# Two attention layers over one context: Gram matrix of each context made in layer 0, kept in DRAM and loaded by layer 1

## What is computed

```python
# layer 0: text = ctx[:, :77], ip = ctx[:, 77:]
text_probs = softmax((x @ Wq) @ (text @ Wk).T * scale)
q_sem = text_probs @ text                       # [q, 512]
sem = q_sem @ ip.T * scale                      # = text_probs @ (text @ ip.T) * scale
fused = scores_ip + 0.5 * sem                   # the same sem for every head
...
# layer 1: text = ctx[:, :252], ip = ctx[:, 252:]
qsem = l2norm(probs_t @ text)                   # per head; probs_t: [h, q, 252]
ip_n = l2norm(ip)
sem = qsem @ ip_n.T
fused = attn_scores + 0.5 * sem
```

## Time and profile before

| | before |
|---|---|
| median of 3 runs | 1670.71 us |
| profiled execution: its span, first to last instruction | 1665.6 us |
| distance of the median from that span | 5.1 us |
| TensorE matmul busy | 1599.7 us (96%), 14248 matmuls |
| VectorE busy | 1376.6 us (83%) |
| ScalarE busy | 992.3 us (60%) |
| GpSimd busy | 844.8 us (51%) |
| moved by DMA | 175.31 MB, 105 GB/s on average |

### The profile page before, as it was taken

The page is one execution under the profiler, slowest core; times in us unless marked ns, Lnnn a source line. Parts: engine busy times, 40 slices in busy tenths (PEclk is TensorE's granted clock), DMA queues, the critical chain, the costliest instruction groups (busy, mean ns, idle before and its releaser), DMA issues.

```text
span 1665.6 us, 42402 instructions
## 1 busy us (share of the span) xinstructions
PE 1599.7 (96%) x14248; PEld 1424.2 (86%) x14248; DVE 1376.6 (83%) x3937; ACT 992.3 (60%) x2044; POOL 844.8 (51%) x789
## 2 busy tenths in 40 slices
PE   6999999999999999998989999999999999999986
PEld 5888888888888888788878998989998989998866
DVE  4688788888888888867879998999999998998874
ACT  3455565555556555655656666666666666666651
POOL 3224422222222323424767676777667776777662
PEclk9999999999999999999999999999999999999988
DMA  8334444444444444542323332333233323332201
GB/s 223 97 105 121 129 121 124 124 129 125 120 129 124 124 128 122 144 123 75 112 88 87 100 95 80 102 106 99 66 109 102 100 67 101 101 103 63 79 22 43
DMA packets 204225, 175.31 MB, mean 105 GB/s; under 512 B 45441, under 2 KB 203531, under 8 KB 204011
## 3 DMA queue, kind: packets, MB, share of 16 engines
q1 hardware_dynamic: 204010, 172.60, 35.8%
HBM read 112.13 MB, written 60.38 MB: 104 GB/s over the span
## 4 chain that ended last, share of the span: by engine, by line
PE 88%; DVE 6%; issue 3%; DMA 1%; SPq 1%; ACT 1%; POOL 0%; DVEq 0%; POOLq 0%; ACTq 0%
PE MISC L103 26%; PE GP L103 20%; PE NAT L265 10%; PE TR L278 8%; PE PV L324 5%; PE PV L309 4%; PE PV L306 3%; PE PV L327 2%; PE MISC L227 2%; PE MISC L367 1%; DVE ZP L895 1%; PE MISC L368 1%; PE MISC L466 1%; DVE TMP L779 1%; PE MISC L388 1%
## 5 line engine op out<-in xcount | busy, mean ns | idle before, releaser
L540 ACT ACTIVATE P<-TA 128x512 f32<-128x512 f32 x320 | 202.6, 633 | 279.4 <-DVE TA L888 278.0
L984 POOL TENSOR_TENSOR ZS<-ZP 128x256 f32<-128x256 f32 x267 | 255.4, 957 | 210.4 <-DVE ZP L895 209.0
L265 PE MATMUL NAT<-KS,QS 65*128 65x256 f32 x1280 | 300.1, 317 | 3.6 <-DMA KS<-qk_parts 2.1
L103 PE MATMUL GP<-PH,GH 128*128 128x256 f32 (+1 forms) x960 | 248.8, 288 | 20.9 <-DVE ZP L895 19.9
L278 PE MATMUL TR<-QS,KS 69*128 69x256 f32 (+1 forms) x1280 | 259.9, 285 | 4.6 <-DMA QS<-max_rows 2.5
L783 DVE TENSOR_REDUCE MX<-NAT 128x2 f32<-128x504 f32 x320 | 216.6, 677 | 51.3 <-PE NAT L265 46.9
L901 DVE SCALAR_TENSOR_TENSOR PM<-P,PH 128x512 f32<-128x512 f32 x320 | 255.3, 798 | 0.0
L215 POOL TENSOR_TENSOR PARTS<-QKF,PARTS 112x508 fp32r<-112x508 f32 (+3 forms) x93 | 119.3, 1283 | 265.1 <-ACT PARTS L568 263.2
L265 PEld LDWEIGHTS NAT<-KS,QS 65*128 65x128 f32 x1280 | 201.2, 192 | 56.9 <-issue 42.1
L103 PE MATMUL GP<-PH,GL 128*128 128x256 f32 (+1 forms) x960 | 243.0, 281 | 0.0
L543 ACT ACTIVATE P<-TR 128x512 f32<-128x512 f32 x320 | 192.7, 602 | 74.3 <-PE TR L278 71.3
(11 more groups left out here) (253 smaller groups left out, 3886.9 us busy)
## 6 DMA issues: line engine op xcount, KB each, us to landing
QS<-qk_parts SPq DMA_DIRECT2D x480, 64.0 KB
KS<-qk_parts SPq DMA_DIRECT2D x480, 64.0 KB
qk_parts<-PARTS SPq DMA_DIRECT2D x128, 224.0 KB, 2.8
CT<-in_ctx_t SPq DMA_DIRECT2D x32, 512.0 KB, 3.9
qk_parts<-PARTS SPq DMA_DIRECT2D x64, 192.0 KB, 2.4
XT<-in_x_t SPq DMA_DIRECT2D x48, 112.0 KB, 2.6
XT<-x_t SPq DMA_DIRECT2D x48, 112.0 KB, 2.4
XB<-in_x SPq DMA_DIRECT2D x16, 320.0 KB, 4.1
```

Source lines behind the costliest of these rows:

```text
L103: ins = e.matmul(out, lhs, rhs, start=(n == 0), stop=(n == len(pairs) - 1))
L265: ins = e.matmul(NAT[s % 2][:, i * T:(i + 1) * T], QS[0:KQ, h, i * 128:(i + 1) * 128], KS[0:KQ, h, :], start=True, stop=True)
L540: e.activation(P[:, s % NP, :], TA[:, s % 2, :], ACT.Exp, scale=SCALE).then_inc(q["exp"], 1)
L984: e.tensor_tensor(ZS[s % NZ][:, :], ZP[:, s % 2, 0:S], ZP[:, s % 2, S:2 * S], ALU.add).then_inc(q["zs"], 1)
```

## The change

Layer 0 makes the whole Gram matrix of its context, from CTS, in two products at offsets 3 and 8 in place of G0 (the second product with all 128 rows). ScalarE takes G0's block out of the first one, scaled by 0.5, and copies all three blocks into a new SBUF tile GR (128 x 3 x 128 float32, 192 KB). At offset 9 GR is stored to DRAM. In layer 1 the two products and the scaling of CT are gone. GR is loaded at offset 6; at offset 9 VectorE scales its last four columns (gx); at offsets 12 and 13 ScalarE and VectorE make VB's columns, GH and GL as before, with GR as the source in place of PSUM. The context loads of the sync queue wait for the Gram products in place of G0; the first one of layer 1 waits for the last product of layer 0, at offset 8. The declarations of the DRAM tensor and of the semaphores are left out below.

```diff
@@ -38,9 +38,9 @@
...
 
-AT0 = dict(q=(-9, -5, -1), k=(-8, -4, 0), spill=(-7, -3, 1), x_in=-22, xts=-14, c_in=-15, cts=-1, tl=2, norm=3, g0=3, tpt=4,
+AT0 = dict(q=(-9, -5, -1), k=(-8, -4, 0), spill=(-7, -3, 1), x_in=-22, xts=-14, c_in=-15, cts=-1, tl=2, norm=3, gram=(3, 8), g_out=9, tpt=4,
            sem=6, v=(10, 14, 18), xb_in=53, num=44, hst=49, htl=50, om=(64, 67), y=(65, 68), yt=(72, 73), out=69, out_t=74)
-AT1 = dict(q=(0, 4, 9), k=(1, 5, 10), spill=(2, 6, 11), x_in=-22, xts=-9, c_in=-15, ctn=-4, cts=-2, v=(6, 8), gr=(12, 13), gl=(13, 14),
+AT1 = dict(q=(0, 4, 9), k=(1, 5, 10), spill=(2, 6, 11), x_in=-22, xts=-9, c_in=-15, cts=-2, v=(6, 8), g_in=6, gx=9, gr=(12, 13), gl=(13, 14),
            kbd=9, scm=17, vip_in=38, vip=46, cmb=48, inv=56, f0=60, f2=61, sub=64, tx=65, sum=68, f1=71,
@@ -142,6 +142,7 @@
...
     ZS = [sb(f"ZS{k}", [128, S]) for k in range(3)]
+    GR = sb("GR", [128, 3, 128])
 
@@ -410,11 +411,17 @@
...
                 ins.then_inc(q["tl"], 1)
-            b = of0(t, AT0["g0"])
-            if b is not None:
-                k, free = take(("g0", b), (q["g0s"], b + 1), t)
-                e.wait_ge(*free)
-                product(e, k[0:NT0, 0:NI0], [(CT[:, c, 0:NT0], CT[:, c, NT0:T]) for c in range(KC)]).then_inc(q["g0"], 1)
+            for n, off in enumerate(AT0["gram"]):
+                b = of0(t, off)
+                if b is not None:
+                    k, free = take(("gram", b, n), (q["grw"], 2 * b + n + 1), t)
+                    if free:
+                        e.wait_ge(*free)
+                    e.wait_ge(q["ct_lo"], b + 1)
+                    if n == 0:
+                        product3(e, k[:, 0:T], CTS, CTS, lambda x, c: x[:, c, 0:128], lambda y, c: y[:, c, :], KC).then_inc(q["gram"], 1)
+                    else:
+                        product3(e, k[:, 0:128], CTS, CTS, lambda x, c: x[:, c, 128:T], lambda y, c: y[:, c, 128:T], KC).then_inc(q["gram"], 1)
             b = of0(t, AT0["tpt"])
@@ -445,15 +452,6 @@
...
                     product3(e, k[0:w_n, 0:C], CTS, WV, lambda x, c: x[:, c, t0:t0 + w_n], lambda y, c: y[:, c, :], KC).then_inc(q["vm"], 1)
-            for n, off in enumerate(AT1["gr"]):
-                b = of1(t, off)
-                if b is not None:
-                    k, free = take(("gr", b, n), (q["gl"], 3 * b + (2, 3)[n]), t, 1.4)
-                    e.wait_ge(*free)
-                    if n == 0:
-                        product3(e, k[:, 0:T], CTS, CTS, lambda x, c: x[:, c, 0:128], lambda y, c: y[:, c, :], KC).then_inc(q["gr"], 1)
-                    else:
-                        product3(e, k[0:N2, 0:128], CTS, CTS, lambda x, c: x[:, c, 128:NT], lambda y, c: y[:, c, 128:T], KC).then_inc(q["gr"], 1)
             b = of1(t, AT1["scm"])
@@ -622,9 +620,9 @@
...
                 e.wait_ge(q["vm"], of_v(B + b))
-                if b:
-                    e.wait_ge(q["gr"], 2 * b)
-                e.wait_ge(q["ctn"], b + 1)
+                if b == 0:
+                    e.wait_ge(q["gram"], 2 * B)
+                e.wait_ge(q["c_in"], 16 * (B + b + 1))
                 e.copy(CTS[0][:, :, :], CT[:, :, :]).then_inc(q["ct_hi"], 1)
@@ -635,11 +633,19 @@
...
                              accum_out=TPM[:, 2, 1:2]).then_inc(q["texp"], 1)
-            b = of0(t, AT0["g0"])
-            if b is not None:
-                e.wait_ge(*((q["stm"], b) if b else (q["g0z"], 1)))
-                e.wait_ge(q["g0"], b + 1)
-                e.mul(G0[:, NT0:T], ring.bank["g0", b][0:NT0, 0:NI0], 0.5).then_inc(q["g0s"], 1)
+            for n, off in enumerate(AT0["gram"]):
+                b = of0(t, off)
+                if b is not None:
+                    k = ring.bank["gram", b, n]
+                    e.wait_ge(q["gram"], 2 * b + n + 1)
+                    if n == 0:
+                        e.wait_ge(*((q["stm"], b) if b else (q["g0z"], 1)))
+                        e.mul(G0[:, NT0:T], k[0:NT0, NT0:T], 0.5).then_inc(q["g0s"], 1)
+                        if b:
+                            e.wait_ge(q["g_out"], 16 * b)
+                        e.copy(GR[:, 0:2, :], k[:, 0:T].rearrange("p (n t) -> p n t", n=2)).then_inc(q["grw"], 1)
+                    else:
+                        e.copy(GR[:, 2, :], k[:, 0:128]).then_inc(q["grw"], 1)
             b = of0(t, AT0["tpt"])
@@ -673,20 +679,19 @@
...
                 if b is not None:
-                    k, p = ring.bank["gr", b, n], b % 2
-                    w_n, c0 = ((128, NT), (N2, N2))[n]
+                    p, w_n = b % 2, (128, N2)[n]
                     if n == 0:
...
                             e.wait_ge(q["gp"], H * (b - 1))
-                    e.wait_ge(q["gr"], 2 * b + n + 1)
-                    e.copy(VB[0:w_n, p, n, :, D + 1:D + 5], k[0:w_n, c0:c0 + 4].unsqueeze(1).broadcast_to([w_n, H, 4])).then_inc(q["vc"], 1)
+                    e.wait_ge(q["gx"], b + 1)
+                    e.copy(VB[0:w_n, p, n, :, D + 1:D + 5], GR[0:w_n, n + 1, N2:128].unsqueeze(1).broadcast_to([w_n, H, 4])).then_inc(q["vc"], 1)
                     if n == 0:
-                        e.copy(GH[:, p, 0, :], k[:, 0:128]).then_inc(q["gh"], 1)
-                        e.mul(GH[:, p, 1, 0:N2], k[:, 128:NT], 2.0).then_inc(q["gh"], 1)
+                        e.copy(GH[:, p, 0, :], GR[:, 0, :]).then_inc(q["gh"], 1)
+                        e.mul(GH[:, p, 1, 0:N2], GR[:, 1, 0:N2], 2.0).then_inc(q["gh"], 1)
                     else:
-                        e.copy(GH[0:N2, p, 2, 0:N2], k[0:N2, 0:N2]).then_inc(q["gh"], 1)
+                        e.copy(GH[0:N2, p, 2, 0:N2], GR[0:N2, 2, 0:N2]).then_inc(q["gh"], 1)
             if t == WV0[0]:
@@ -737,16 +742,16 @@
...
                 if b is not None:
-                    k, p = ring.bank["gr", b, n], b % 2
+                    p = b % 2
                     if n == 0 and b >= 2:
...
                     if n == 0:
-                        e.tensor_tensor(GL[:, p, 0, :], k[:, 0:128], GH[:, p, 0, :].bitcast(F32), ALU.subtract).then_inc(q["gl"], 1)
-                        e.scalar_tensor_tensor(GL[:, p, 1, 0:N2], k[:, 128:NT], 2.0, GH[:, p, 1, 0:N2].bitcast(F32), ALU.mult,
+                        e.tensor_tensor(GL[:, p, 0, :], GR[:, 0, :], GH[:, p, 0, :].bitcast(F32), ALU.subtract).then_inc(q["gl"], 1)
+                        e.scalar_tensor_tensor(GL[:, p, 1, 0:N2], GR[:, 1, 0:N2], 2.0, GH[:, p, 1, 0:N2].bitcast(F32), ALU.mult,
                                                ALU.subtract).then_inc(q["gl"], 1)
                     else:
-                        e.tensor_tensor(GL[0:N2, p, 2, 0:N2], k[0:N2, 0:N2], GH[0:N2, p, 2, 0:N2].bitcast(F32), ALU.subtract).then_inc(q["gl"], 1)
+                        e.tensor_tensor(GL[0:N2, p, 2, 0:N2], GR[0:N2, 2, 0:N2], GH[0:N2, p, 2, 0:N2].bitcast(F32), ALU.subtract).then_inc(q["gl"], 1)
             for i in range(2):
@@ -870,13 +875,13 @@
...
                                 ALU.mult).then_inc(q["kbd"], 1)
-            b = of1(t, AT1["ctn"])
+            b = of1(t, AT1["gx"])
             if b is not None:
...
                     e.wait_ge(q["rn"], 3)
-                e.wait_ge(q["c_in"], 16 * (B + b + 1))
-                e.tensor_tensor(CT[:, :, NT:T], CT[:, :, NT:T], RN[:, 1, NI * b:NI * b + NI].unsqueeze(1).broadcast_to([128, KC, NI]),
-                                ALU.mult).then_inc(q["ctn"], 1)
+                e.wait_ge(q["g_in"], 16 * (b + 1))
+                e.tensor_tensor(GR[:, 1:3, N2:128], GR[:, 1:3, N2:128], RN[:, 1, NI * b:NI * b + NI].unsqueeze(1).broadcast_to([128, 2, NI]),
+                                ALU.mult).then_inc(q["gx"], 1)
             s = t
@@ -1019,8 +1024,6 @@
...
             for b in both(t, AT0["cts"], AT1["cts"]):
-                if b > B:
-                    e.wait_ge(q["gr"], 2 * (b - B))
                 if b:
@@ -1202,16 +1205,27 @@
...
                 load_x(B + b)
+            b = of0(t, AT0["g_out"])
+            if b is not None:
+                e.wait_ge(q["grw"], 2 * b + 2)
+                e.dma_start(gram_h[b], GR[:, :, :]).then_inc(q["g_out"], 16)
+            b = of1(t, AT1["g_in"])
+            if b is not None:
+                e.wait_ge(q["g_out"], 16 * B)
+                if b:
+                    e.wait_ge(q["gl"], 3 * b)
+                    e.wait_ge(q["vc"], 2 * b)
+                e.dma_start(GR[:, :, :], gram_h[b]).then_inc(q["g_in"], 16)
             b = of0(t, AT0["c_in"])
...
                 e.wait_ge(q["ct_lo"], b)
-                e.wait_ge(q["g0"], b)
+                e.wait_ge(q["gram"], 2 * b - 1)
                 load_ctx(b)
...
                 if b == 0:
-                    e.wait_ge(q["g0"], B)
+                    e.wait_ge(q["gram"], 2 * B)
                 load_ctx(B + b)
...
```

More of the change, by code:

```diff
@@ L116, in whole, with build @@
     return w_dr.rearrange("(k p) n -> p k n", p=128)
-def build(nc, ctx, a, parts_h, sel_h, rows_h, vall, x1, x1_t, out):
+def build(nc, ctx, a, parts_h, sel_h, rows_h, vall, gram_h, x1, x1_t, out):
     def tiles(stack):
@@ L193, in build @@
```

(7 more changed lines are left out.)

## The result

The changed kernel takes 1699.0 us (median of 6 runs, 1692.6 to 1704.1) where the kernel before, timed beside it, takes 1668.6 (6 runs). The profiled execution is the shortest of the six, 1692.6 us. The ratio is 1.0189, with a 95% interval from 1.0169 to 1.0208: slower by 1.9%. I had forecast 1666.4 us in a range from 1650 to 1678. It is my rival 2, which I had folded together with rival 4 into a chance of 0.13.

The account below looks back on a forecast made before the run. TensorE was taken to bound layer 0, TensorE and nearly VectorE layer 1. Layer 0's +16.2 and layer 1's -20.5 us gave -4.3 on a 1665.6 us span; plus 5.1 to the median, 1666.4 us, range 1650 to 1678.

Parts of the forecast that it names:

- rival 2: Layer 1: the new TensorE stall lowers its clock; +20 us, 1690 us; chance 0.13 together with rival 4.
- rival 4: Layer 1: ScalarE's copies wait for a load landing later than three slots (8 us); no relief; chance 0.13 with rival 2.
- Layer 0: Added Gram products less the filled XB wait: +1.0 us in each of 13 contexts, +16.2 us in total.
- the cover: Layer 0: CTSL ready 2.6 us before its product, ScalarE's extra copies absorbed at 59% share; both costed at nothing.
- The chain through ZP: Layer 1, slots 12 to 14: VectorE's ZP delays GP, so of 2.87 us removed 1.35 survives; new stall 1.26 us.
- GL's reading of SBUF: Layer 1: two SBUF inputs may let GpSimd delay GL; gain between 0.5 and 1.35 us a context, taken as 1.05.
- rival 3: Layer 1: GpSimd blocks every GL, 0.5 us gained a context; +4.4 us in total, 1675 us; chance 0.09.
- The clock: Layer 1: TensorE's clock assumed to hold through the new stall, citing one 1.95 us wait at clock 1.00.
- The price of a drop: Layer 1: some 6.7 us at the 1.2 GHz level was priced at 3.4 us.
- The 5.1 us between span and median: Whole kernel: the earlier median stood 5.1 us above the profiled span; that distance was kept and added to 1661.3.
- Rival 1: Layer 1: TensorE alone sets the pace; -29.7 us, 1641 us; chance 0.26 with its half-way cases.
- The seam: Between layers: the first layer-1 context load waits for slot 8 instead of 3; 0 to 3 us once, taken as 0.

Follow-up runs that it names:

- `l0_side`: Kernel before, with layer 0 making and storing the Gram matrix unused while layer 1 still computes its own: 1681.3 us against 1665.2, ratio 1.0079.
- `fill`: Changed kernel, with layer 1's two Gram products issued again at slots 12 and 13, results thrown away: 1678.8 us, ratio 1.0063 to the kernel before.
- `parts`: Changed kernel, with GH and GL made in layer 0 by ScalarE and VectorE, stored, and loaded in layer 1: 1673.4 us against 1667.4 for the kernel before.
- `l1_side`: Kernel before, with layer 1's Gram products removed and a stand-in of the same size loaded; layer 0 unchanged: 1682.4 us, ratio 1.0092.
- `before_v`: Kernel before, with only layer 1's value products cut in halves at slots 6, 8, 12 and 13: 1687.7 us against 1668.0, ratio 1.0116.
- `parts_v`: `parts` plus layer 1's value products in halves at slots 6, 8, 12 and 13: 1658.7 us, ratio 0.9947 to the kernel before.
- `split_v`: Changed kernel, with layer 1's two value products in halves at slots 6, 8, 12 and 13: 1652.4 us against 1665.2 for the kernel before.

## Why the prediction was wrong, point by point

- **Layer 0** (+1.0 a context, the wait for XB gone): right, 44.2 against 43.2. CTSL and ScalarE's queue had the cover that I gave them. `l0_side` as a whole costs 13 us by its ratio and 16 by its medians, where my sum had 16.2 for this layer.
- **The chain through ZP** (2.87 us removed, new stall 1.26 us): right in mechanism and low in size. The stall is 1.90 us: the two GL of slot 13 take 0.52 and 0.81 us instead of 0.29 and 0.28, and most of these 0.76 us lies in the chain.
- **GL's reading of SBUF**: the mis-sized term. I took it near its free end, from the mean excess of PM, 0.12 us. Measured is 0.52, 0.81 and 0.81 us for 0.29, 0.28 and 0.29. PM's mean was the wrong figure to go by, since it mixes 286 operations that weren't held with 32 that were, by 0.7 to 1.2 us each; the MN at 2.02 us was the right one. Why the 286 weren't held stays open. The two steady contexts without a drop of the clock take 54.2 us, a gain of 0.4: the 0.5 us end of rival 3. With that term right, and the clock at its level, the sum would have been my rival 3, 1675 us; `fill`, with the clock held, is at 1678.8. The Trainium skill's page "SBUF — State Buffer", section "Who interferes with whom", names this case (two SBUF inputs against a GpSimd read), and the trace agrees with it in GL, 43 operations of 48; of PM, which has two SBUF inputs as well, only one in ten was held.
- **The clock** (rival 2): the step that failed. I took it that the clock holds through the new stall, on one row, a wait of 1.95 us at 783.94 with the clock at 1.00. I had treated a stall that comes once as evidence for one that comes 13 times; two of 13 contexts have the same luck here (1256 and 1536). The granted clock's stretches at half its value were named in the prediction as a sign that it is wrong, and they came. `fill` and `parts` show the cause by two different ways: close the hole with work or by shortening VectorE's chain, and the stretches at 1.2 GHz go. What decides whether a given hole does it stays open. Neither the length of the wait nor the little that TensorE did around it decides alone: 1.9 us with 2.10 of 4 us busy brought the clock down in 11 of 13 contexts, while 2.51 us with 1.49 of 4 busy didn't (`l1_side`), and neither did 1.3 us with 2.69 busy, in every context (`before_v`), nor waits up to 0.5 us with 3.45 busy in the window shown (`parts`).
- **The price of a drop** was too high: contexts with 3.4 us at 1.2 GHz take some 55.7, with 6.8 us 57.0, without 54.2, so 1.5 and 2.8 us, not 3.4. Over the twelve steady contexts of the profiled execution that makes 20.3 us (670.7 less 12 x 54.2); on rival 3's 1675 it gives 1695. The median, 1699.0, is 4 us more; the five other executions show a mean granted clock of 0.958 to 0.966 against the profiled one's 0.967, so they spent more time at the lower level, but where isn't recorded.
- **The 5.1 us between span and median** aren't a fixed distance: the profiled execution of the changed kernel, 1692.6 us, stands 1.8 us above its span, and the median 8.2.
- **Rival 1** (TensorE alone) fell; even `parts_v`, with nothing of GL left, takes 52.1 to 52.2, and 54.6 - 2.87 = 51.7 was its claim. **Rival 4** (the load is late) fell for the changed kernel; it cost 1.2 us at most, three times, in the faster `split_v`.
- **The seam**: taken as 0 of 0 to 3 us. The span up to the end of layer 0 is 9.3 us longer. Up to layer 0's second context it is 5.8 us shorter (first TR at 94.2 against 100.0), which no term of mine has: in its profiled execution the kernel before spends 13.7 us at 1.2 GHz before 80 us, the changed one none, and whether that is the change or chance isn't shown. From there it is 15.1 us longer. The waits of TensorE for QS from the row maxima (690 to 900) are 3.7 us after and 2.0 before. How the 3.8 us more in the first three contexts of layer 1 divide between these waits and the clock (two stretches at 1.2 GHz between 804 and 824, 10 us together, where the kernel before has none) I haven't taken apart.

## What to carry to other kernels

Where engines run in step, slot by slot, look at what fills each slot before work is taken out of it: of the 2.87 us of removed matmuls a context gives back 0.4, as VectorE sets the pace there and its GL is held by GpSimd, and the hole that they leave costs 1.5 to 2.8 where the clock falls. Take the work out on both engines, or move needed work into the empty slots: the change alone is 1.9% slower than the kernel before; with the value products in halves it is 0.7% faster, and with the halves and the parts made by GpSimd in layer 0 it is 1.5% faster. Before taking a mean for a price, look at the longest of the group. And an operation whose second input moves from PSUM to SBUF must be priced, until its own rows say otherwise, at nearly its length plus the rest of the GpSimd operation beside it (GL of 0.28 us ended 0.15 us after that operation), not at its own length.

## What the hardware showed that I had not expected

- A wait of 1.9 us in a TensorE that is otherwise busy (95% of the span), coming back every 54 to 57 us, was followed by 3.4 or 6.8 us at 1.2 GHz in 11 of 13 contexts. Waits of 1.3 us in every context (`before_v`) and of up to 0.5 us (`parts`) were followed by none, and a single one of 2.51 us (`l1_side`) wasn't either.
- 46 us of useless matmuls made a kernel some 20 us faster (`fill` against the changed kernel, each by its ratio to the kernel before).
- VectorE operations of 0.28 and 0.29 us (the second and third GL) took over 0.5 us, 0.81 in the median, in 30 of 32 cases, and ended 0.15 us after the GpSimd operation beside them. PM, with two SBUF inputs as well, was held in 32 of 320.
